# Gates and the experts' output biases as three bf16 numbers each, 48 rows in one product, the biases loaded in the middle of the attention

## The reference

```python
x = x + a                                   # the mixture's own attention
gates = jax.nn.softmax(x @ Wg + bg, axis=-1)
hmid = jax.nn.relu(jnp.einsum('bsh,ehd->bsed', x, W1) + b1)
eout = jnp.einsum('bsed,edh->bseh', hmid, W2) + b2
y = jnp.einsum('bse,bseh->bsh', gates, eout)
```

## Time and profile before

| | |
|---|---|
| runs | 1026.92 us median of 3 (1026.81 to 1027.49) |
| profiled execution | 1026.7 us, its span 1025.0 us |
| busy, share of the span | PE 90%, PEld (weight loads) 74%, DVE 61%, ACT 55%, POOL 28% |
| chain that ended last, by engine | PE 74%, ACT 10%, DVE 6%, DMA 3%, SP's queue 3%, issue 3%, POOL 1% |
| granted clock of PE, mean | 0.959 |

### The profile page before, as it was taken

The page is one execution under the profiler, slowest core; times in us unless marked ns, Lnnn a source line. Parts: engine busy times, 40 slices in busy tenths (PEclk is TensorE's granted clock), DMA queues, the critical chain, the costliest instruction groups (busy, mean ns, idle before and its releaser), DMA issues.

```text
span 1025.0 us, 20305 instructions
## 1 busy us (share of the span) xinstructions
PE 927.5 (90%) x7910; PEld 761.2 (74%) x7910; DVE 621.7 (61%) x1968; ACT 564.7 (55%) x951; POOL 282.1 (28%) x357
## 2 busy tenths in 40 slices
PE   3679998989989999999999999999999996999960
PEld 2445554555679898988989888898898885889960
DVE  7787787787469685454654636555455855852226
ACT  2287778786776555445455546546445563654420
POOL 6946154120201111023203232022322003077660
PEclk9688999989999999999999999999999998999995
DMA  5433443434771000000000000000000013023218
GB/s 157 123 126 113 151 145 99 135 118 162 193 172 65 1 1 2 1 1 19 3 2 21 1 22 1 6 18 1 22 1 17 6 42 103 14 73 94 77 35 248
DMA packets 85243, 66.39 MB, mean 65 GB/s; under 512 B 8098, under 2 KB 75672, under 8 KB 85148
## 3 DMA queue, kind: packets, MB, share of 16 engines
q1 hardware_dynamic: 80724, 56.80, 18.8%
q0 software_dynamic: 4352, 8.28, 2.5%
q10 hardware_dynamic: 72, 0.02, 0.0%
HBM read 33.76 MB, written 31.59 MB: 64 GB/s over the span
## 4 chain that ended last, share of the span: by engine, by line
PE 74%; ACT 10%; DVE 6%; DMA 3%; SPq 3%; issue 3%; POOL 1%; POOLq 0%; ACTq 0%; DVEq 0%
PE psum L1414 25%; PE psum L1391 19%; PE psum L1236 4%; PE psum L1174 3%; PE psum L1466 2%; PE psum L1190 2%; PE psum L1217 1%; PE psum L1144 1%; PE psum L1295 1%; ACT big L2317 1%; PE psum L1338 1%; PE psum L1316 1%; ACT ew L2212 1%; PE psum L1166 1%; PE psum L1250 1%
## 5 line engine op out<-in xcount | busy, mean ns | idle before, releaser
L1414 PEld LDWEIGHTS psum<-ew,big 128*128 128x128 f32 x2560 | 315.7, 191 | 18.7 <-ACT big L2317 3.3
L1414 PE MATMUL psum<-ew,big 128*128 128x128 f32 x2560 | 322.2, 276 | 1.2 <-ACT big L2317 1.0
L2317 ACT ACTIVATE big<-psum,cols 128x512 f32<-128x512 f32 x256 | 174.3, 689 | 174.3 <-PE psum L1391 173.9
L1391 PE MATMUL psum<-parts,q_stack 128*128 128x512 f32 x640 | 219.1, 423 | 2.0 <-ACT big L2324 1.4
L1757 DVE TENSOR_REDUCE maxes<-psum 128x4 f32<-128x1024 f32 (+1 forms) x96 | 113.8, 1217 | 26.1 <-PE psum L1190 25.8
L1391 PE MATMUL psum<-parts,k_stack 128*128 128x512 f32 x320 | 125.9, 393 | 0.0
L2584 POOL DMA_INDIRECT routed<-big,slot_i x64 | 62.8, 981 | 225.3 <-DVE slot_i L2072 180.0
L1883 DVE SCALAR_TENSOR_TENSOR hT<-psum,gates,hT 128x128 f32<-128x128 f32 x256 | 71.8, 344 | 84.8 <-PE psum L1414 84.5
L1391 PEld LDWEIGHTS psum<-parts,q_stack 128*128 128x128 f32 x640 | 106.1, 190 | 13.3 <-ACT big L2324 1.9
L2594 POOL DMA_INDIRECT answers<-hT,to x64 | 62.2, 973 | 69.1 <-DVE hT L2091 50.8
L1391 PEld LDWEIGHTS psum<-parts,k_stack 128*128 128x128 f32 x320 | 60.1, 188 | 13.6
(11 more groups left out here) (381 smaller groups left out, 1535.9 us busy)
## 6 DMA issues: line engine op xcount, KB each, us to landing
q_stack<-q_pieces SPq DMA_DIRECT2D x32, 192.0 KB
k_stack<-k_pieces SPq DMA_DIRECT2D x32, 192.0 KB
routed<-empty_row SPq DMA_DIRECT2D x4, 1040.0 KB, 12.0
big<-routed SPq DMA_DIRECT2D x16, 260.0 KB, 2.9
answers<-gb_tok SPq DMA_DIRECT2D x4, 1024.0 KB, 10.7
q_pieces<-gb_tok SPq DMA_DIRECT2D x16, 192.0 KB, 2.1
k_pieces<-gb_tok SPq DMA_DIRECT2D x16, 192.0 KB, 2.1
x<-in_L_attn_x SPq DMA_DIRECT2D x4, 512.0 KB, 6.3
```

The source lines that it names most:

```text
L1391: last = eng.matmul(bank(i), w1_part(wp, e)[:, fs], parts[2 * xk + xp][:, :], start=n == 0, stop=n == 2)
L1414: last = eng.matmul(psum[:, i, k * C:(k + 1) * C], hid[:, r, f, k * P:(k + 1) * P], ew2[:, e, f, :], start=f == 0, stop=f == FC - 1)
L2317: eng.activation(hid[:, held("hid", "up", n, e, f), f, :], bank(held("bank", "up", n, e, f)), ACT.Relu, bias=col("L0_ffn_b1", e * FC + f)) ...
```

## The change

The gates of a tile and b2 are each cut into three bf16 numbers (a first piece, the rest's first piece, the rest of that), g = g0 + g1 + g2 and b = b0 + b1 + b2. Of the nine products of pieces the six with indices summing to at most 2 are kept (`PAIRS`): 6 x 8 = 48 rows (`PROWS`), each a piece of the gate against a piece of the bias, so one bf16 product over 48 rows gives their sum.

New steps: `b2` on SP, behind the row maxima of batch 8: six DMAs of b2 (8 rows each) into `col_rows`. `ss_c` on DVE, once, behind b2 and `gv_v` 3: a bf16 identity, a selection of the piece for each row, and the 48 rows in bf16. `ss_p` on POOL, per chunk, behind `mg_n`: the gates' pieces, repeated 3, 2 and 1 times, 48 columns a tile. `ss_t` is now four bf16 matmuls with a bf16 identity, behind `ss_p` and `ss_c`; `ss_b` four bf16 products over 48 rows. The b2 load leaves POOL's late loads, whose semaphore is awaited at 7 x 16. The planned costs change with it. The rows of bq and bk, which lay in gT, get a tile of their own.

```diff
+PAIRS = [(g, b) for g in range(3) for b in range(3 - g)]
+PROWS = len(PAIRS) * NE
...
-        one("ss_t", n, "pe:.4 act:.57", [("mg_n", n)] + ([("ss_b", n - 2)] if n >= 2 else []), rank, chain)
-        one("ss_b", n, "pe:1.08 act:.5", [("ss_t", n)], rank, chain)
+        p.step("ss_p", n, work="pool:2", after=[("mg_n", n)] + ([("ss_t", n - 2)] if n >= 2 else []), rank=rank, chain=chain)
+        one("ss_t", n, "pe:.3 act:.57", [("ss_p", n), ("ss_c",)] + ([("ss_b", n - 2)] if n >= 2 else []), rank, chain)
+        one("ss_b", n, "pe:.35 act:.5", [("ss_t", n)], rank, chain)
...
+    p.step("b2", work="sp:3 dma:3", after=[("mrow", B // 2)])
+    p.step("ss_c", work="dve:2.4", after=[("b2",), gated])
...
-        b2 = sb("b2", [NE, C])
+        b2_piece = sb("b2_piece", [PROWS, C], BF16)
+        b2_rows = sb("b2_rows", [PROWS, C], BF16)
+        picks_b2 = sb("picks_b2", [PROWS, 3])
+        ident_b = sb("ident_b", [P, P], BF16)
+        gate_pieces = sb("gate_pieces", [P, 2, CT, PROWS], BF16)
+        gate_rest = sb("gate_rest", [P, 2, CT, NE])
...
+        b2, b2_rest = col_rows[0:PROWS, :], dst_[0:PROWS, :, :].rearrange("p t k -> p (t k)")[:, 0:C]
...
-        gT = sb("gT", [NE, 2, CHUNK])
+        gT = sb("gT", [PROWS, 2, CHUNK], BF16)
...
+            def b2_in_rows():
+                for r in range(len(PAIRS)):
+                    eng.dma_start(b2[NE * r:NE * (r + 1), :], a["L0_ffn_b2"]).then_inc(b2_in, 16)
...
             def ss_t(n):
+                w.wait_ge(*done("ss_p", n))
+                w.wait_ge(*done("ss_c"))
...
-                    last = eng.transpose(psum[0:NE, i, k * P:(k + 1) * P], gates[:, t, :], ident[:, :])
+                    last = eng.matmul(psum[0:PROWS, i, k * P:(k + 1) * P], gate_pieces[:, n % 2, k, :], ident_b[:, :],
+                                      start=True, stop=True)
...
-                    last = eng.matmul(psum[:, i, k * C:(k + 1) * C], gT[:, n % 2, k * P:(k + 1) * P], b2[:, :],
+                    last = eng.matmul(psum[:, i, k * C:(k + 1) * C], gT[:, n % 2, k * P:(k + 1) * P], b2_rows[:, :],
...
+            def ss_c():
+                w.wait_ge(consts, IDENT)
+                eng.tensor_copy(ident_b[:, :], ident[:, :])
+                for b in range(3):
+                    rows_of = [r for r, (_, piece) in enumerate(PAIRS) if piece == b]
+                    for n, r in enumerate(rows_of):
+                        eng.tensor_reduce(picks_b2[:, b:b + 1] if n == 0 else b2_rest[:, n:n + 1], ident[0:PROWS, NE * r:NE * (r + 1)],
+                                          X_AXIS, ALU.add).then_inc(chain.sem, chain.more())
+                    for n in range(1, len(rows_of)):
+                        w.wait_ge(chain.sem, chain.n)
+                        eng.tensor_tensor(picks_b2[:, b:b + 1], picks_b2[:, b:b + 1], b2_rest[:, n:n + 1],
+                                          ALU.add).then_inc(chain.sem, chain.more())
+                w.wait_ge(chain.sem, chain.n)
+                w.wait_ge(b2_in, 16 * len(PAIRS))
+                rest = b2
+                for b in range(3):
+                    eng.tensor_copy(b2_piece[:, :], rest).then_inc(chain.sem, chain.more())
+                    w.wait_ge(chain.sem, chain.n)
+                    if b == 0:
+                        eng.tensor_scalar(b2_rows[:, :], b2_piece[:, :], picks_b2[:, 0:1], None, ALU.mult).then_inc(chain.sem, chain.more())
+                    else:
+                        eng.scalar_tensor_tensor(b2_rows[:, :], b2_piece[:, :], picks_b2[:, b:b + 1], b2_rows[:, :], ALU.mult,
+                                                 ALU.add).then_inc(*((chain.sem, chain.more()) if b == 1 else (sem("ss_c"), 1)))
+                    if b < 2:
+                        eng.tensor_tensor(b2_rest, rest, b2_piece[:, :], ALU.subtract).then_inc(chain.sem, chain.more())
+                        w.wait_ge(chain.sem, chain.n)
+                        rest = b2_rest
...
-                eng.copy(gT[:, n % 2, :], psum[0:NE, held("bank", "ss_t", n), :]).then_inc(sem("ss_t"), 1)
+                eng.copy(gT[:, n % 2, :], psum[0:PROWS, held("bank", "ss_t", n), :]).then_inc(sem("ss_t"), 1)
...
-                eng.dma_start(b2[:, :], a["L0_ffn_b2"]).then_inc(late_in, 16)
...
+            def ss_p(n):
+                r, g = gate_rest[:, n % 2, :, :], gates[:, CT * n:CT * (n + 1), :]
+                w.wait_ge(*done("mg_n", n))
+                if n >= 2:
+                    w.wait_ge(*done("ss_t", n - 2, by="pe"))
+                at = 0
+                for piece in range(3):
+                    times = 3 - piece
+                    mine = gate_pieces[:, n % 2, :, at:at + NE]
+                    last = eng.tensor_copy(gate_pieces[:, n % 2, :, at:at + times * NE].rearrange("p t (r e) -> p t r e", e=NE),
+                                           g.unsqueeze(2).to_broadcast([P, CT, times, NE]))
+                    if piece < 2:
+                        last.then_inc(chain.sem, chain.more())
+                        w.wait_ge(chain.sem, chain.n)
+                        eng.tensor_tensor(r, g, mine, ALU.subtract).then_inc(chain.sem, chain.more())
+                        w.wait_ge(chain.sem, chain.n)
+                    g, at = r, at + times * NE
+                last.then_inc(sem("ss_p"), 1)
```

More of the change, by code:

```diff
@@ L106 @@
     "am_s": ("gates", "pool"), "am_x": ("gates", "pe dve"),
-    "ss_t": ("gates", "pe act"), "ss_b": ("gates", "pe act"),
+    "b2": ("setup", ""), "ss_c": ("gates", "dve"), "ss_p": ("gates", "pool"), "ss_t": ("gates", "pe act"), "ss_b": ("gates", "pe act"),
     "sw": ("split", "act dve"), "sx": ("split", "act dve"),
@@ L772, in build @@
         ew2_in = [semaphore(f"ew2_in{i}") for i in range(2)]
-        raw_in, blk_in, blk_zero = (semaphore(n) for n in ("raw_in", "blk_in", "blk_zero"))
+        raw_in, blk_in, blk_zero, b2_in = (semaphore(n) for n in ("raw_in", "blk_in", "blk_zero", "b2_in"))
         routed_out = [semaphore(f"routed_out{i}") for i in range(2)]
@@ L819, in build @@
         cond_rows = spare[0:CONDS, C:2 * C]
-        col_rows = sb("col_rows", [n_cols - CONDS, P])
+        col_rows = sb("col_rows", [max(n_cols - CONDS, PROWS), P])
         def col(name, i=0):
@@ L881, in build @@
         bet = sb("bet", [P, G2, HD])
-        qk_rows = gT[0:2, :, 0:C]
+        qk_rows = sb("qk_rows", [2, 2, C])
         var, vrs = (sb(name, [P, 2, BPC * TPB * G2]) for name in ("var", "vrs"))
@@ L1115, in cols_ @@
                     w.wait_ge(*c)
-                eng.transpose(psum[:, held("bank", "cols"), 0:n], col_rows[:, :],
+                eng.transpose(psum[:, held("bank", "cols"), 0:n], col_rows[0:n, :],
                               ident[0:n, 0:n]).then_inc(sem("cols", "pe"))
@@ L1266, in po_w @@
                 w.wait_ge(*done("po_t", n))
-                w.wait_ge(late_in, 16 * 8)
+                w.wait_ge(late_in, 16 * 7)
                 for c in cleared("bank", "po_w", n):
@@ L2124, in _ @@
                     "po_x": po_x, "am_x": am_x, "mx_v": mx_v, "mx_s": mx_s, "mx_n": mx_n, "mx_a": mx_a, "vo": vo, "mg_l": mg_l,
-                    "mg_n": mg_n, "sw": sw, "sx": sx, "mix": mix, "ag": ag, "wt": wt, "wc": wc, "blk": blk,
+                    "mg_n": mg_n, "ss_c": ss_c, "sw": sw, "sx": sx, "mix": mix, "ag": ag, "wt": wt, "wc": wc, "blk": blk,
                     "la_v": la_v, "la_r": la_r, "la_m": la_m, "la_h": la_h, "la_o": la_o, "la_a": la_a, "la_2": la_2, "la_x": la_x, "rt_s": rt_s,
@@ L2597, in send @@
                         oob_is_err=False).then_inc(answer_out[k], 16)
-            mine = {"masks": masks, "late": late, "ln_p": ln_p, "rest": rest, "cut": cut, "gv_a": gv_a, "gv_w": gv_w, "gv_v": gv_v, "am_s": am_s, "blk": blk, "gam": gam_, "tab": tab,
+            mine = {"masks": masks, "late": late, "ln_p": ln_p, "rest": rest, "cut": cut, "gv_a": gv_a, "gv_w": gv_w, "gv_v": gv_v, "ss_p": ss_p, "am_s": am_s, "blk": blk, "gam": gam_, "tab": tab,
                     "la_g": la_g, "rt_d": rt_d, "send": send}
```

4 lines of the change are left out of this document (1 added, 3 removed).

## The result

| | before | after |
|---|---|---|
| median of five runs each | 1026.92 us (1026.63 to 1028.94) | 1017.40 us (1015.75 to 1018.57) |
| ratio | 1 | 0.9895, 95% interval 0.9878 to 0.9912 |
| profiled execution, its span | 1026.7, 1025.0 us | 1017.07, 1015.3 us |
| PE busy | 927.5 us | 922.0 us |
| granted clock of PE, mean | 0.959 | 0.959 |

PE's busy time falls by 5.5 us and the span by 9.7, so some 4 us are not PE's work at all.

The account below looks back on a forecast made before the run. The wait for the last fill's landing at 296.79 us was taken as the bound before it, PE from 299.5 to 800 us. 1026.7 - 5.2 (PE work) + 0.5 (DVE block) = 1022.0 us, range 1018.5 to 1028.0.

Parts of the forecast that it names:

- Order: PE order redrawn behind batch 8's maxima; idle from 410 to 860 us may move either way: zero, 2.5 us of width.
- PE's work: Bias product and gates' transposes on PE: 1.70 us per chunk becomes 0.96, saving 0.74; over seven chunks 5.2 us.
- my price for the borders: Changes between fp32 and bf16 groups on PE: 0.16 us ahead and 0.08 us behind, per step.
- the transposes gain nothing: Gates' transposes on PE cost 0.48 us in bf16 for 0.43 before; the whole saving is the bias product's.
- Chunk 0: Its bias product at 274.6 us lies ahead of the fills' end at 296.79 us, so only seven chunks count.
- POOL's pieces at nothing: ss_p on POOL, some 1.3 us per chunk, is covered by experts' products on PE, so it costs nothing.
- The loads on SP and the late load on POOL at nothing: Six SP loads take 3.6 us but batch 11's stacking has lead; one POOL load fewer gains nothing: zero.
- The DVE block at 0.5: ss_c on DVE, from 233 us: 4.8 us of work, mostly caught up in idle gaps; cost 0.5, bounds 0 and 4.8.
- Given back: Attention ends late by most of ss_c's 4.8 us, or new order idles 3 to 4 us more: 1026.3 us, chance 0.20.
- slower, PE waits for POOL: PE waits at ss_t for POOL's pieces, some 1.5 us at each of eight waits: 1034 us; chance 0.13, including worse last-chunk orders.
- bf16 saves only the lower bound: PE's bf16 groups are bound by loading weights and borders, saving only 2.5 us: 1024.7 us, chance 0.12.
- More: borders cost nothing, or the new order idles less: On PE, free borders save 8.5 us, or the new order idles less: 1018.2 us, chance 0.08.

Follow-up runs that it names:

- the two runs with 1.0 in the plan: Unchanged kernel's instructions, bias product planned at 1.0 instead of 1.08 us on PE, run on two chips: 1025.52 us, ratio 0.9967, and 1029.16 us, ratio 0.9963.
- the fills issued 6.4 us later: Changed kernel with ss_c planned at cost 0 instead of 2.4 us: 1048.58 us, ratio 0.9875, beside the changed kernel's 1049.69 us, 0.9887, on the same chip.
- the doubled block: Changed kernel computing the bias rows (ss_c on DVE) twice in a row: 1053.00 us, ratio 0.9919, beside 0.9887 for the changed kernel.
- the order of before: Changed kernel's instructions in exactly the unchanged kernel's orders, new steps put in when their inputs are there: 1072.07 us, ratio 1.0031 to the unchanged kernel.
- experiment 1: Order and work taken apart: unchanged kernel's instructions in the changed kernel's orders, 1061.89 us, ratio 0.9943; changed instructions in the unchanged orders, 1072.07 us, 1.0031.

## Why the prediction was wrong, by its steps

**The step that failed** is "Order": "That can move the idle times on PE ... either way; I give it zero and 2.5 us of width". The order is worth 2.4, 5.0, 6.1 and 10.6 us on four chips, always on the good side. On the chip of the prediction it wasn't measured alone; what the work leaves there is 9.5 - 4.5 = 5.0 us (6.3 by the ratio). I looked at the 7.9 idle microseconds between 800 and 860 us and took the redrawn order for noise around them. Most of them are the wait of 6.86 us, which the new order keeps (6.81). What it changes stands just behind 860 us, where I read no rows: a choice between two ways of laying one turn, worth 3.4 and 3.8 us by the two runs with 1.0 in the plan. The kernel before was on the bad side of that choice. Nor did I price the order's effect on layer 1 (119.2 to 120.2 us) and behind the last matmul (34.0 to 32.3 us).

**PE's work was right.** Forecast 0.74 us a chunk, measured 0.72 by the rows. A bf16 matmul of 128 columns costs 0.324 / 4 = 0.081 us and not my 0.06, while the borders cost 0.14 to 0.18 us a step and not 0.24; the two errors cancel. The Trainium skill (TensorE: Matmul & The Clock Gate, "Back-to-back issue gap") had the 81 ns, and the trace agrees for the bias product (the turning takes 0.335 / 4 = 0.084 us); the estimate from it, 0.56 us a step, came out too high (0.48 and 0.50) only through my price for the borders. That the transposes gain nothing held: 0.48 for 0.43.

**Chunk 0** I had left out, since time saved before the fills' landing would run into the wait for them. That the landing isn't a bound that hands its lateness on in full was shown by the fills issued 6.4 us later with no measured loss. PE's wait for the gate tile behind them is 1.1 to 6.3 us in the traces that have it, and it doesn't follow the landing: 2.5 us with a landing at 294.07 us, 1.8 with one at 298.80 (changed kernel, and the one with the doubled block, on one chip). So I count all eight chunks by the rows, 8 x 0.72 = 5.8 us; the runs, with 4.4 and 4.8 us, can't tell that from seven.

**POOL's pieces at nothing: right**, with the condition named. Without the planned cover I had said 1.3 us a chunk; the order of before shows 5.9 us over seven waits, 0.84 each. **The loads on SP and the late load on POOL at nothing: right**, at 2.17 us instead of 3.6.

**The DVE block at 0.5: the number holds as far as the traces tell, the reason doesn't.** No run leaves the block's instructions out, so the number rests on the missing wait. I said the gaps behind it would catch a block up, since a third of DVE is idle. The doubled block shows that they don't: the second 3.3 us are handed on in full, by the one step behind it that PE waits for, and not by the maxima, where I had looked. That the single block came to nothing was luck of its size: it took 3.3 us and not the 4.8 of my sum, and by the doubled block 4.8 us would have cost some 1.5 us (an estimate, 4.8 - 3.3). The small instructions follow each other after 0.12 us on the mean and not 0.20, the wide ones after 0.25 and not 0.33.

**The rivals.** "Given back" and "slower, PE waits for POOL" did not happen, but both mechanisms exist: the second was seen in before's orders (ratio 1.0031), the first with the doubled block. "bf16 saves only the lower bound" fell with the rows. Nearest was the fourth, "More: borders cost nothing, or the new order idles less", 1018.2 us at 0.08: by its second half, which deserved a price of its own.

**Open.** Why the same order is worth 2.4 us on one chip and 10.6 on another, and with it what of the 5.0 us above the 3.4 to 3.8 is the order's at all. One part shows on the chip of experiment 1, where the order was worth 6.1 us: the gap is 26.8 us in before's orders and 21.0 in after's, 5.8 us and not 3.7, of which 4.1 lie behind the long wait. The chip with 10.6 us has no trace in before's orders. The planned end moves by 7.2 us, of which 8 x 0.83 = 6.6 are the products' lower cost, so the order's share can't be read from there either.

## What to carry to other kernels

Where a planner writes the order of the instructions, a change has two effects, and they can be measured apart: old instructions in the new order, new instructions in the old. Before crediting an edit, change a planned cost by a tenth of a microsecond or so without touching an instruction; the spread it gives (here 3.4 us, nearly as much as the edit's work) is the least width that the order deserves in a forecast, since on one chip it was worth 10.6 us here; and if the kernel at hand is on the bad side of a choice, that width isn't centred on zero. And an engine's idle share doesn't say what a block on it costs: look for the step that stands behind it in its order and for who waits for that, and count with the clock that PE loses by the wait.

## What the runs showed of the hardware that was not expected

In the mixture a group of another type or row count costs its neighbours: mostly 0.08 to 0.10 us ahead of it and 0.05 to 0.10 behind (0.02 to 0.03 where `up` products of 512 columns follow), for fp32 products of 8 rows as for bf16 ones of 48. Between two groups of the attention (lines 1217 and 1236, chunk 0 of before, at 274.6 us) the product of 8 rows costs its neighbours nothing. An fp32 product over 8 rows and 128 columns takes 1.08 / 4 = 0.27 us, as an fp32 transpose of 128 columns takes 0.11. Five POOL instructions of 32 to 96 elements take 0.21 to 0.26 us each, nearly whatever their size, and 0.06 to 0.09 us lie between each two.

A wait on PE can cost more than its length at its place: with the doubled block 3.28 us of waiting put PE 5.4 us behind, because its granted clock stood at the lower level from 244.2 to 251.1 us.

The chips of the five batches ran the unchanged kernel in 1029.62 to 1068.32 us. For one pair the traces say where: before's instructions in after's orders had a span of 1027.8 us on one and 1051.1 on another, and of the 23.3 us between them 19.3 lie between the first product of layer 1 and the last matmul (120.3 and 139.6 us). There PE is idle for 16.5 us instead of 1.7, and its granted clock is 0.95 instead of 1.00. Why its releasers are late on the one chip isn't known.
